# Splitting the late expert weights inside the sampling stage of a fused audio tower

## The chip, the cores and the metric

The kernel runs on one core of a Trainium2 chip. The metric is the device time of one execution in microseconds (us), lower is better; beside it stands the profile of one execution. TensorE multiplies matrices, ScalarE (ACT) and VectorE (DVE) work on columns, GpSimd (POOL) does elementwise work on SBUF, and SyncE (SP) issues DMAs from one queue in program order.

## The reference

```python
h = L0_tok(x)                              # 32 x 166 tokens of 128
h = h + L0_attn(layernorm(h))              # a linear recurrence
h = h + L0_ffn(layernorm(h))               # 16 experts of 512, top 2; an expert's tokens are averaged
h = h + L1_attn(layernorm(h))              # 8 heads; 38 sampled keys choose 25 queries
h = h + L1_ffn(layernorm(h))               # 64 experts of 256, top 42, gelu

# L0_ffn, after the top 2 of the gate (mask, routing_w):
h = silu(einsum('td,efd->tef', x, w1))
h_mean = einsum('tef,te->ef', h, mask) / max(counts, 1)
out = einsum('tk,tkd->td', routing_w, einsum('ef,edf->ed', h_mean, w2)[top_idx])
# L1_ffn, for each expert e of 64:
y = gelu(x @ w1[e] + b1[e]) @ w2[e] + b2[e]     # weighted by comb[:, e] and summed
```

## The kernel before

One core runs five stages one after the other, with a barrier between them: the recurrence, the first mixture (it shares a block with the recurrence), the statistics and sampling of the sparse attention (one block), the attention proper, and the second mixture. Activations lie with their 128 features on the partitions and the 5312 tokens on the columns.

**The weights of the second mixture.** Its 64 experts are held as f16 pairs: a weight is rounded, and what is left of it, scaled up, goes into a second f16 (called splitting below). Experts come in four groups of 16. A group is 8 pieces of 1024 columns (4 for each of the two matrices). Group 0 stays in SBUF; groups 1 to 3 are split early, written to a DRAM buffer (`expert_factors`, kept), and read back in the last stage. Splitting one piece is four operations on GpSimd: round, subtract, scale, add (lines 2202 to 2210 and 2266 to 2274). `ExpertWeights` splits groups 0 and 1 (16 pieces) in the block of statistics and sampling: three pieces beside the statistics, and one after each of the diagonals of chunks 1 to 13. `LateWeights` splits groups 2 and 3 (16 pieces) on GpSimd beside the first mixture. Both have two buffers for raw columns and two for made pairs. The SP queue issues a piece's load as soon as the raw buffer has been read, and its write to DRAM (`sync_keep`) as soon as it is split.

**The first mixture** (`FirstMixture`). The routing has written each token's row to the slots of its two experts in DRAM. 43 tiles of 384 slots follow. For each, SP issues one transposing DMA into a ring of 8 (line 1346), and TensorE makes four blocks of 128 hidden features, each two matmuls of 384 columns (line 1403). Two blocks (768 columns of PSUM) are a set, and four sets are in flight. ScalarE takes silu in place (line 1368), VectorE sums each block over its columns (line 1374). SP also issues, between the transposing loads, the four quarters of the second matrix (after tiles 3, 8 and 13) and, in two of every five tiles, a late load and a late keep, and it waits for GpSimd ahead of each keep. After the last tile come some 30 us of small products that make the outputs.

**Statistics and sampling.** 16 chunks of 332 tokens. The statistics stage makes means and variances chunk by chunk; `rstd` of the first half is ready first. Then for each chunk c GpSimd makes a diagonal of `rstd` (line 1255), TensorE spreads it with one product (line 1261, `pe_spread`), and VectorE normalises. TensorE's work for chunk c is: sampled keys of c, the query and key products of chunk c + 1, the spread of chunk c + 2, and then four times a token-major product of chunk c + 1 and the sampled scores of c. ScalarE copies: query, key, and for each of the four quarters of a chunk three copies of 128 columns (line 1643); its work on chunk c + 1 falls into TensorE's work on chunk c. The sampled keys of c need all four of its quarters copied. Three lines set the order between GpSimd and TensorE:

```python
for c in range(NC):                                  # GpSimd
    norm.pool_diagonal(pool, c, c % 2, stats)        # waits for spread of c - 2
    if 1 <= c <= end - first: k.expert_weights.pool_pieces(pool, first + c - 1, first + c)
```

The block ends for all engines when the last has come to its end, and GpSimd has some constants to make behind its loop (lines 1608 to 1622).

Of the kernel before, what the change touches and what calls it, by code (L numbers as in the profile page):

```python
# [904 lines left out]
def recurrence(nc, k, tables, routing):  # L905
# [8 lines left out]
    with ExitStack() as ctx:  # L914
# [47 lines left out]
        @block.sync  # L962
        def _(sp):
            routing.sync_start(sp)
            for p in range(NC):
                if p >= 2:
                    sp.wait_ge(w_wide, p - 1)
                sp.dma_start(wst[:, p % 2, :], a["w1"][:, p * piece:(p + 1) * piece]).then_inc(raw_in[p % 2], 16)
            routing.sync_fill(sp)
            mixture.sync(sp, y_ready)  # L970

        @block.gpsimd
        def _(pool):
# [19 lines left out]
            mixture.pool(pool)  # L993
# [279 lines left out]
class FirstMixture:  # L1273
# [7 lines left out]
    W2_AT = (3, 8, 13)  # L1281
    KEEP_FROM, KEEP_EVERY = 4, 5

    def __init__(self, nc, k, routing, w_in, w_out, ut, state_of, xc, xsn):
        def sem(name):
# [4 lines left out]
        self.late = LateWeights(nc, k, w_in.rearrange("p a b c d -> p (a b c d)").rearrange("p (j n) -> p j n", j=2),  # L1290
                                w_out.rearrange("p a b c d -> p (a b c d)")[:, 0:2 * PIECE].bitcast(F16).rearrange("p (j q n) -> p j q n", j=2, q=2),
                                states[:, 0:PIECE])
        self.hsum = states[:, PIECE:PIECE + FC * E0 * E0].rearrange("p (f x) -> p f x", f=FC)
        self.ym = states[:, PIECE + FC * E0 * E0:PIECE + FC * E0 * E0 + 128]
        self.part = xc.rearrange("p q c -> p (q c)")[:, 0:NST * FC].rearrange("p (n f) -> p n f", f=FC)
        self.part_t = xsn.rearrange("p q c -> p (q c)")[0:NST, 0:FC * 128]
        self.xt = ut.rearrange("p g i c -> p (g i c)")[:, 0:self.RING * ST].bitcast(F16).rearrange("p (n m t) -> p n m t", n=self.RING, m=2)
# [15 lines left out]
        k.w0_down = k.weights[:, 1].bitcast(F32).rearrange("p a b -> p (a b)")  # L1313
        self.w2 = k.w0_down.rearrange("p (e f d) -> p e f d", e=E0, f=FC)
# [10 lines left out]
    def sync_down(self, sp, q):  # L1325
        es = slice(q * E0 // 4, (q + 1) * E0 // 4)
        sp.dma_start(self.w2[:, es], self.k.a["w2"][:, es]).then_inc(self.k.w2_in, 16)

    def sync(self, sp, outputs_made):
        k, routing, late = self.k, self.routing, self.late  # L1330
        sp.wait_ge(outputs_made, NC)
        late.sync_load(sp, 0)
        late.sync_load(sp, 1)
        sp.wait_ge(k.w0_split, NC)
        self.sync_down(sp, 0)
# [7 lines left out]
        for j in range(NST):  # L1343
# [7 lines left out]
        while late.kept < late.count:  # L1351
# [1483 lines left out]
```

## Time and profile before

| | us |
|---|---|
| median of 3 runs | 2064.61 (2061.93 to 2066.79) |
| the profiled execution, its own time | 2067.39 |
| its span in the trace | 2065.7 |
| first mixture, first tile product to last sum | 283.3 to 397.7 |
| its small products | 397.7 to 428.8 |
| statistics of the third norm | 428.8 to 457.3 |
| sampling | 457.3 to 583.8 |
| attention proper | 583.8 to 718 |
| second mixture | 718 to 2065.7 |

The span is what the trace covers of one execution; the execution's own time is 1.7 us longer. All times in the trace are counted from the start of the span. A wait is shown with the engine and the line that ended it.

### The profile page before, as it was taken

To read this page: it belongs to the slowest core of one execution; us is meant where nothing else is said; L and a number is where in the kernel's file an instruction comes from. 1 tells how busy PE (TensorE), PEld (TensorE's weight loads), DVE (VectorE), ACT (ScalarE), POOL (GpSimd) and SP (SyncE) were. 2 spreads that over 40 slices of the span, in tenths; PEclk is the share of its full clock that TensorE was granted. 3 is DMA by queue.
4 is the path that set the end of the run, shared out by engine and by line. 5 is a ranking of instruction groups with operands and counts; after the bars stand their busy time and mean duration, and the time that the engine had idled before them with its cause. 6 is when DMAs were issued, how large, how long until landed. Compare 5 with 4: busy or idle time off the path is not lost.

```text
span 2065.7 us, 50535 instructions
## 1 busy us (share of the span) xinstructions
PE 1870.1 (91%) x17038; PEld 1349.7 (65%) x17038; DVE 1676.4 (81%) x4833; ACT 1378.0 (67%) x2149; POOL 1455.0 (70%) x1098
## 2 busy tenths in 40 slices
PE   7887436789989978999999999999999999999998
PEld 5555213456669855777777777777777777777776
DVE  5887736555678788899999999999999999999998
ACT  4134525424435545888888888888888888888886
POOL 2216679559800032888888888888888888888887
PEclk9998768789989965999999999999999999999999
DMA  3011289523200010000000200000100000000000
GB/s 93 21 35 63 81 246 257 124 67 94 90 1 1 22 63 1 2 2 0 0 0 3 82 2 0 0 0 35 49 1 0 0 0 2 2 10 11 10 11 19
DMA packets 64334, 77.56 MB, mean 38 GB/s; under 512 B 38932, under 2 KB 47028, under 8 KB 62132
## 3 DMA queue, kind: packets, MB, share of 16 engines
q1 hardware_dynamic: 61364, 70.08, 11.7%
q0 software_dynamic: 2816, 5.45, 0.8%
q8 instruction: 94, 1.54, 0.3%
q14 instruction: 60, 0.49, 0.1%
HBM read 42.97 MB, written 24.08 MB: 32 GB/s over the span
## 4 chain that ended last, share of the span: by engine, by line
PE 58%; DVE 3%; issue 2%; ACT 1%; POOL 0%; ACTq 0%; DVEq 0%; POOLq 0%
PE bank L2679 30%; PE bank L2662 28%; DVE m_work L2553 1%; DVE m_best L2550 1%; DVE m_work L2544 0%; PE bank L2632 0%; DVE m_ut L1269 0%; ACT m_h L2485 0%; DVE m_best L2543 0%; DVE m_ex L2555 0%; DVE h L2591 0%; DVE m_red L2556 0%; DVE m_row L2536 0%; POOL m_diag L1255 0%; ACT m_hidden L2482 0%
## 5 line engine op out<-in xcount | busy, mean ns | idle before, releaser
L2679 PEld LDWEIGHTS bank<-weights,m_h 128*128 128x128 f16 x10752 | 649.6, 98 | 194.4 <-DVE hc L2582 82.6
L2430 POOL TENSOR_TENSOR m_h<-m_hidden,m_h 128x896 f16<-128x896 f32 x384 | 725.9, 1890 | 32.0
L2679 PE MATMUL bank<-weights,m_h 128*128 128x128 f16 x10752 | 724.6, 219 | 10.7 <-POOL m_h L2430 2.1
L2582 DVE SCALAR_TENSOR_TENSOR hc<-bank,m_shares,hc 128x128 f32<-128x128 f32 x2688 | 727.2, 342 | 4.3 <-PE bank L2679 4.3
L2482 ACT ACTIVATE m_hidden<-bank,m_b 128x896 f32<-128x896 f32 x384 | 386.9, 1007 | 197.6 <-PE bank L2662 197.5
L2567 DVE TENSOR_TENSOR m_h<-bank,m_h 128x896 f16<-128x896 f32 x384 | 419.2, 1092 | 116.8 <-ACT m_h L2485 116.7
L2428 POOL TENSOR_SCALAR m_h<-m_hidden 128x896 f16<-128x896 f32 x384 | 360.8, 939 | 117.9 <-ACT m_hidden L2482 99.5
L2662 PE MATMUL bank<-m_u_first,weights 128*128 128x448 f16 (+1 forms) x1536 | 417.8, 354 | 5.5 <-DVE h L2591 5.5
L2662 PE MATMUL bank<-m_u_second,weights 128*128 128x448 f16 (+1 forms) x1536 | 417.7, 354 | 0.0
L2479 ACT ACTIVATE bank<-bank,m_b 128x896 f32<-128x896 f32 x384 | 377.6, 983 | 0.6 <-PE bank L2662 0.6
L2485 ACT ACTIVATE m_h<-bank 128x896 f16<-128x896 f32 x384 | 349.1, 909 | 0.0
L2662 PEld LDWEIGHTS bank<-m_u_second,weights 128*128 128x128 f16 x1536 | 150.8, 98 | 141.4 <-issue 2.0
L699 POOL DMA_INDIRECT expert_slots<-weights,ro_slot x88 | 88.9, 1010 | 76.5 <-DVE weights L839 50.6
L1403 PE MATMUL bank<-lru_ut,weights 128*128 128x384 f16 x344 | 74.1, 373 | 74.5 <-DMA lru_ut<-expert_slots 60.0
L1374 DVE TENSOR_REDUCE lru_xc<-bank 128x2 f32<-128x768 f32 x86 | 77.2, 950 | 67.4 <-ACT bank L1368 67.3
L2662 PEld LDWEIGHTS bank<-m_u_first,weights 128*128 128x128 f16 x1536 | 118.2, 98 | 8.1 <-DVE h L2591 6.4
L1368 ACT ACTIVATE bank<-bank 128x768 f32<-128x768 f32 x86 | 64.7, 798 | 82.6 <-PE bank L1403 82.1
L2399 POOL MEMSET m_row<- 128x96 f32 x1 | 0.2, 178 | 157.0 <-POOLq L1827 157.0
L1403 PEld LDWEIGHTS bank<-lru_ut,weights 128*128 x344 | 37.3, 108 | 110.7 <-issue 99.9
L980 POOL TENSOR_TENSOR lru_diag<-ident,rstd 128x332 f32<-128x332 f32 x16 | 13.5, 858 | 65.3 <-PE bank L1147 41.3
L1711 DVE TENSOR_REDUCE at_peak<-bank 83x8 f32<-83x304 f32 x64 | 30.0, 468 | 35.4 <-PE bank L1769 35.2
L1751 PE MATMUL bank<-at_w_qk,at_ut 128*83 128x384 f32 x128 | 52.9, 501 | 0.0
(359 smaller groups left out, 2153.9 us busy)
## 6 DMA issues: line engine op xcount, KB each, us to landing
weights<-expert_factors SPq DMA_DIRECT2D x12, 1024.0 KB, 8.8
lru_w_in<-e_w_dram SPq DMA_DIRECT2D x16, 512.0 KB, 4.5
expert_factors<-lru_w_out SPq DMA_DIRECT2D x16, 512.0 KB, 4.3
ew_raw<-e_w_dram SPq DMA_DIRECT2D x16, 512.0 KB, 3.9
weights<-w_dram SPq DMA_DIRECT2D x16, 256.0 KB, 2.8
weights<-w_dram SPq DMA_DIRECT2D x4, 1024.0 KB, 6.6
expert_factors<-ew_made SPq DMA_DIRECT2D x8, 512.0 KB, 3.0
xs<-x_dram SPq DMA_DIRECT2D x4, 996.0 KB, 11.8
```

The lines of the kernel that those rows point to most:

```text
L699: g.indirect_dma_start(out=self.k.slots, out_offset=bass.IndirectOffsetOnAxis(ap=self.slot[0:size, q, n:n + 1], axis=0), in_=self.u_tok[0: ...
L1374: v.tensor_reduce(self.part[:, j // PARTS, j % PARTS * FP:(j % PARTS + 1) * FP], self.set_banks(j), X, ALU.add).then_inc(self.summed, 1)
L1403: last = t.matmul(self.set_banks(n)[:, f % FP], self.w0_parts[m][:, bass.ds(expert * FF0 + f * 128, 128)], self.xt[:, j % RING, m], start= ...
L2428: g.tensor_scalar(h1[:, x, 0], hidden[:, x], 1.0 - SHARE, 1.0, ALU.mult, ALU.mult).then_inc(first_of[1], 1)
L2430: g.tensor_tensor(h1[:, x, 1], hidden[:, x], h1[:, x, 0], ALU.subtract).then_inc(second_of[1], 1)
L2479: sc.activation(banks0(x), banks0(x), ACT.Gelu, bias=b1[:, bass.ds(grp * GE + e, 1), 0]).then_inc(gelu[0], 1)
L2482: sc.activation(two(hidden[:, x % 2]), banks1, ACT.Gelu, bias=b1[:, bass.ds(grp * GE + e, 1), 1]).then_inc(gelu[1], 1)
L2485: sc.activation(two(h0[:, x, 0]), banks0(x), ACT.Copy, scale=1.0 - SHARE).then_inc(first_of[0], 1)
L2567: v.tensor_tensor(two(h0[:, x, 1]), banks0(it), two(h0[:, x, 0]), ALU.subtract).then_inc(second_of[0], 1)
L2582: last = v.scalar_tensor_tensor(acc[:, m * TW:(m + 1) * TW], y[q][:, (n - start) * TW:(n - start + 1) * TW], shares[:, m, e:e + 1], acc[:, ...
L2662: last = t.matmul(bank[:, q], k.weights[:, grp % 2, m, at], uu[:, bass.ds(tb * WB + q * HW, HW)], start=(m == 0), stop=(m == 1))
L2679: last = t.matmul(y[q][:, (n - start) * TW:(n - start + 1) * TW], factors[:, m, n * TW:(n + 1) * TW], k.weights[:, grp % 2, 2 + m, at], st ...
```

## The change

Four things change.

1. The 16 late pieces leave GpSimd and the first mixture. They become 32 pieces of 512 columns (`PIECES` goes from 4 to 8 for both classes), two in each of the 16 chunks of the sampling. ScalarE rounds and scales (two operations of 512 columns, after the copies of quarters 1 and 3), VectorE adds (one operation, ahead of the maxima of quarters 0 and 2). They have four raw and four made buffers, two chunks deep, which lie where the squares of the statistics were.
2. The early pieces, now 32 of 512 columns, stay on GpSimd with two buffers each, and all lie in the sampling: two after the diagonal of each chunk from 1 to 15, and two behind the loop. The statistics have none.
3. The second matrix of the first mixture is loaded at once, ahead of the fills of the slots, into four places that are free by then.
4. Of the 86 sets of the first mixture, every sixth (14) is summed by ScalarE, as it takes silu, block by block with an accumulator; VectorE skips it.

The SP queue of the sampling block is rewritten. The core of the diff:

```diff
 # FirstMixture
+    BY_ACT = 6
+    def act_sums(self, n):
+        return n % self.BY_ACT == self.BY_ACT - 1
@@ act
             act.wait_ge(self.up, j + 1)
-            self.nc.scalar.activation(self.set_banks(j), self.set_banks(j), ACT.Silu).then_inc(self.silu, 1)
+            if self.act_sums(j):
+                for f in range(self.FP):
+                    at = j % self.PARTS * self.FP + f
+                    last = self.nc.scalar.activation(self.set_banks(j)[:, f], self.set_banks(j)[:, f], ACT.Silu,
+                                                     accum_out=self.part[:, j // self.PARTS, at:at + 1])
+            else:
+                last = self.nc.scalar.activation(self.set_banks(j), self.set_banks(j), ACT.Silu)
+            last.then_inc(self.silu, 1)
@@ sync
-            if j in self.W2_AT:
-                self.sync_down(sp, 1 + self.W2_AT.index(j))
-            if j >= self.KEEP_FROM and (j - self.KEEP_FROM) % self.KEEP_EVERY in (0, 2):
-                late.sync_keep(sp)
 # sampling block, SP
-                k.expert_weights.sync_pieces(sp, *PIECES_N3)
-                k.expert_weights.sync_pieces(sp, *PIECES_SAMPLE)
+                early, late = k.expert_weights, k.late_weights
+                for s in range(2):
+                    early.sync_load(sp, s)
+                sp.wait_ge(stats.var, NC + DEEP)
+                for i in range(4):
+                    late.sync_load(sp, i)
+                for c in range(NC):
+                    for s in range(2):
+                        late.sync_load(sp, 2 * c + 4 + s)
+                    for s in range(2):
+                        late.sync_keep(sp, 2 * c - 2 + s)
+                    for s in range(2):
+                        early.sync_keep(sp, 2 * c - 2 + s)
+                        early.sync_load(sp, 2 * c + 2 + s)
...
 # sampling block, GpSimd
-                k.expert_weights.pool_pieces(pool, *PIECES_N3)
                 for c in range(NC):
                     norm.pool_diagonal(pool, c, c % 2, stats)
-                    if 1 <= c <= end - first:
-                        k.expert_weights.pool_pieces(pool, first + c - 1, first + c)
+                    if c:
+                        k.expert_weights.pool_pieces(pool, PER_CHUNK * (c - 1), PER_CHUNK * c)
+                k.expert_weights.pool_pieces(pool, PER_CHUNK * (NC - 1), PER_CHUNK * NC)
-PIECES = 4
+PIECES = 8
+PIECES_POOL, PIECES_LATE = (0, 2 * GROUP), (2 * GROUP, NG * GROUP)
+PER_CHUNK = 2
 # LateWeights, new
+    def sync_load(self, sp, i):
...
+        if i >= 4:
+            sp.wait_ge(self.raw_read, i - 3)
+        start = n // GROUP * GE * HC * 128 + n % PIECES * PIECE
+        sp.dma_start(self.raw[:, i % 4, :], src[:, start:start + PIECE]).then_inc(self.raw_in[i % 4], 16)
+    def act_piece(self, act, c, j, s):
+        b = 2 * j + s
+        act.wait_ge(self.raw_in[b], 8 * c + 16 - 8 * j)
+        if not isinstance(c, int) or c >= 2:
+            act.wait_ge(self.kept_out[b], 8 * c - 8 * j)
+        self.nc.scalar.activation(self.made[:, b, 0], self.raw[:, b], ACT.Copy).then_inc(self.rounded, 1)
+        if not isinstance(c, int) or c:
+            act.wait_ge(self.split, 2 * c + s - 1)
+        self.nc.scalar.activation(self.wide[:, s], self.raw[:, b], ACT.Copy, scale=1.0 / SHARE).then_inc(self.raw_read, 1)
+    def dve_piece(self, dve, c, j, s):
+        b = 2 * j + s
+        dve.wait_ge(self.rounded, 2 * c + s + 1)
+        dve.wait_ge(self.raw_read, 2 * c + s + 1)
+        self.nc.vector.scalar_tensor_tensor(self.made[:, b, 1], self.made[:, b, 0], 1.0 - 1.0 / SHARE, self.wide[:, s], ALU.mult,
+                                            ALU.add).then_inc(self.split, 1)
```

The waits of the early pieces are as before: `ExpertWeights.sync_load(n)` waits until piece n - 2 has been subtracted, `sync_keep(n)` (from n = 16 on, the second group) until piece n is split, and GpSimd's piece n (from n = 18 on) until the keep of piece n - 2 has landed.

## Rows read from the trace of the kernel before

**Rows 1.** The first line of the page.
```profile
span 2065.7 us, 50535 instructions
```

**Rows 2.** Busy time by stretch: stretch, length, engines, clock, DMA share, GB/s.
```profile
283.30:397.70 114.40, 74.07 (x344) 37.26 (x344) 77.16 (x86) 64.69 (x86) 95.66 (x61) 0.84 0.96 238
...
428.80:457.30 28.50, 20.99 (x155) 16.87 (x156) 15.61 (x31) 9.18 (x19) 21.42 (x16) 0.84 0.35 102
...
457.30:583.80 126.50, 122.59 (x495) 75.16 (x493) 76.15 (x218) 53.42 (x226) 99.13 (x75) 0.97 0.25 79
```

**Rows 3.** Timeline of the DMA queue SP, first mixture: start, length, what.
```profile
330.41 0.38 SPq L2253 DMA_DIRECT2D expert_factors<-lru_w_out  x1
...
330.92 3.74 SPq L1346 DMA_TRANSPOSE lru_ut<-expert_slots  x2
...
337.44 4.24 SPq L1346 DMA_TRANSPOSE lru_ut<-expert_slots  x3
...
343.47 0.38 SPq L2253 DMA_DIRECT2D expert_factors<-lru_w_out  x1
```

**Rows 4.** Timeline of the first mixture, its tiles back to back.
```profile
283.29 7.67 PE L1403 MATMUL bank<-lru_ut,weights 128*128 128x384 f16 x32 [36.04 <-DMA lru_ut<-expert_slots]
...
287.35 4.44 ACT L1368 ACTIVATE bank<-bank 128x768 f32<-128x768 f32 x6 [0.48 <-PE bank L1403]
...
309.67 2.77 PE L1403 MATMUL bank<-lru_ut,weights 128*128 128x384 f16 x16 [3.09 <-DMA lru_ut<-expert_slots]
...
335.70 9.69 DVE L1374 TENSOR_REDUCE lru_xc<-bank 128x2 f32<-128x768 f32 x11 [0.32 <-ACT bank L1368]
```

**Rows 5.** Lines of ScalarE before the first mixture: busy, mean ns, idle before.
```profile
L764 ACT ACTIVATION_READ_ACCUMULATOR weights<-weights 128x1 f32 x44 | 8.5, 193 | 0.0
```

**Rows 6.** The transposing loads, line 1346: ns min/median/max, first and last start.
```profile
L1346 SPq DMA_TRANSPOSE lru_ut<-expert_slots x43: 1205/1347/2764, 280.2 to 389.6; - x43
```

**Rows 7.** Timeline, from the statistics to the first sampling chunk.
```profile
455.00 1.44 POOL L1255 TENSOR_TENSOR at_diag<-ident,rstd 128x332 f32<-128x332 f32 x2
...
455.89 2.55 PE L1261 MATMUL bank<-at_diag,ones 128*128 128x332 f32 x4 [4.96 <-POOL at_diag L1255]
```

**Rows 8.** Timeline of chunks 8 and 9 of the sampling, ScalarE and TensorE.
```profile
525.07 0.27 ACT L1643 ACTIVATE at_kx<-bank 83x128 f32<-83x128 f32 x1
...
527.06 0.72 PE L1261 MATMUL bank<-at_diag,ones 128*128 128x332 f32 x2
...
532.41 0.27 ACT L1643 ACTIVATE at_kx<-bank 83x128 f32<-83x128 f32 x1
```

**Rows 9.** Timeline of GpSimd and SP in the same chunks.
```profile
528.05 0.74 POOL L1255 TENSOR_TENSOR at_diag<-ident,rstd 128x332 f32<-128x332 f32 x1
...
528.12 0.38 SPq L2183 DMA_DIRECT2D expert_factors<-ew_made  x1
...
535.28 0.74 POOL L1255 TENSOR_TENSOR at_diag<-ident,rstd 128x332 f32<-128x332 f32 x1
```

**Rows 10.** Lines of GpSimd: a tensor_tensor of 512 columns.
```profile
L163 POOL TENSOR_TENSOR lru_on_diag<-ident,lru_factor 128x512 f32<-128x512 f32 x4 | 4.0, 1042 | 17.9 <-DVE lru_factor L263 17.9
```

**Rows 11.** DMA issues of the page: KB each, median us to landing.
```profile
weights<-w_dram SPq DMA_DIRECT2D x16, 256.0 KB, 2.8
...
expert_factors<-ew_made SPq DMA_DIRECT2D x8, 512.0 KB, 3.0
```

**Rows 12.** The same splitting of 512 columns in the recurrence: ScalarE, VectorE.
```profile
L1008 ACT ACTIVATE weights<-weights 128x512 f32<-128x512 f32 x16 | 9.9, 616 | 5.9 <-DVE weights L1092 5.9
...
L1092 DVE SCALAR_TENSOR_TENSOR weights<-weights x16: 676/683/1146, 101.7 to 224.0; 128x512 f16<-128x512 f16 x16
```

**Rows 13.** Timeline, end of the sampling block and start of the attention.
```profile
551.14 0.15 POOL L1608 IOTA at_uline<- 83x25 f32 x1
...
555.69 4.14 POOL L1622 TENSOR_SCALAR_AFFINE_SELECT at_expand<-at_expand 128x3200 bf16<-128x3200 bf16 x1
...
583.88 0.32 PE L2030 MATMUL bank<-ch_rank,at_expand 128*100 128x166 bf16 x2 [0.32 <-PEq L1534]
```

More of the change, by code:

```diff
@@ L992, in _ @@
             mixture.pool_clear(pool)
-            mixture.pool(pool)
         @block.scalar
@@ L1326, in sync_down, with sync_second, sync @@
         es = slice(q * E0 // 4, (q + 1) * E0 // 4)
-        sp.dma_start(self.w2[:, es], self.k.a["w2"][:, es]).then_inc(self.k.w2_in, 16)
-    def sync(self, sp, outputs_made):
-        k, routing, late = self.k, self.routing, self.late
+        sp.dma_start(self.w2[q], self.k.a["w2"][:, es]).then_inc(self.k.w2_in, 16)
+    def sync_second(self, sp, outputs_made):
         sp.wait_ge(outputs_made, NC)
[L1332 to L1335, printed above, removed]
+        sp.wait_ge(self.k.w0_split, NC)
+        for q in range(4):
+            self.sync_down(sp, q)
+    def sync(self, sp):
+        k, routing = self.k, self.routing
         sp.wait_ge(routing.rows_made, 1)
@@ L1358, in pool_clear @@
         g.memset(self.ym[:], 0.0).then_inc(self.cleared, 1)
-    def pool(self, pool):
-        for i in range(self.late.count):
-            self.late.pool_piece(pool, i)
     def act(self, act):
@@ L1592, in _ @@
                 sp.dma_start(w_o[:], a["wo"]).then_inc(small_in, 16)
-                k.expert_weights.sync_pieces(sp, *PIECES_N3)
-                k.expert_weights.sync_pieces(sp, *PIECES_SAMPLE)
+                early, late = k.expert_weights, k.late_weights
[12 more added lines that the diff above has]
+                        early.sync_load(sp, 2 * c + 2 + s)
+                for s in range(2):
+                    late.sync_keep(sp, 2 * NC - 2 + s)
+                    early.sync_keep(sp, 2 * NC - 2 + s)
+                late.sync_kept(sp)
+                early.sync_kept(sp)
             @block.gpsimd
@@ L2183, in sync_keep, with sync_kept @@
         sp.dma_start(self.k.kept[n // GROUP - 1, :, 2 * mat:2 * mat + 2, cols], self.made[:, n % 2]).then_inc(self.k.kept_out[n % 2], 16)
-    def sync_pieces(self, sp, first, end):
-        self.sync_load(sp, first)
-        for n in range(first, end):
-            if n + 1 < end:
-                self.sync_load(sp, n + 1)
-            self.sync_keep(sp, n)
-        if end == 2 * GROUP:
-            for p in range(2):
-                sp.wait_ge(self.k.kept_out[p], 16 * GROUP // 2)
+    def sync_kept(self, sp):
+        for p in range(2):
+            sp.wait_ge(self.k.kept_out[p], 16 * GROUP // 2)
     def pool_pieces(self, pool, first, end):
```

101 lines of the change are left out of this document (46 added, 55 removed).

## The prediction, made before the change was run

> **What bounds the kernel now.** I read the stages first, by busy time in each stretch: three of them carry the change [rows 2]. The first mixture takes 114.4 us, and no compute engine that it needs is full in it (TensorE 74, VectorE 77, ScalarE 65); only GpSimd, whose work there is the late pieces, is busy for 96. The timeline of the DMA queue shows why: two keeps later, five tiles later, 13.06 us have gone by [rows 3], so 2.61 us a tile and 43 tiles in 112. SP waits for GpSimd's split ahead of each keep, and the next transposing loads stand behind that wait. The stage goes by GpSimd, through SP's program order. Fed back to back its own engines are faster: 11 sums of VectorE in 9.69 us, 0.87 a set; 6 silus of ScalarE in 4.44 us, 0.73 a set; 16 products in 2.77 us, 0.69 a set [rows 4].
>
> The sampling is TensorE's: 122.6 of 126.5 us [rows 2]. Call K(c) the moment when ScalarE has copied the last quarter of chunk c, S(c) the spread of chunk c. K(8) is 525.34, S(10) is 527.06, K(9) is 532.68 [rows 8]: so K to S 1.7, S to the next K 5.6, a chunk 7.34. GpSimd does a diagonal and a 1024 piece in 7.23 us and never stops [rows 9]; it keeps up because SP has nothing else to do than to serve it.
>
> **First mixture.** Without GpSimd's pieces five sets in six cost ScalarE 0.73, the sixth two activations of 384 columns (0.5 each, between half of a set's and the 0.62 of 512 columns [rows 12]) and two reads of the accumulator at 0.19 [rows 5]: 1.4. That is 5.05 for six, 0.84 a set, 72 us for 86. VectorE has 72 sets at 0.87, 63 us. The transposing loads cost SP 1.35 each, 58 us [rows 6]. ScalarE is the bound. The first 32 products took 7.67 us where the warm rate makes 5.5 [rows 4]; that start, 2.1 us, stays. 74 us against 114.4: **-40 us**. Bounds: 0.78 a set (-45), and 0.9 (-35). The early second matrix goes at some 225 us, while SP waits for the routing: nothing, and nothing is lost if it doesn't, since the matrix is wanted last.
>
> **Statistics.** TensorE stood 4.96 us for the first diagonals, which GpSimd reached only at 455.00, behind its third piece [rows 7]. This piece goes away: **-6 us** (5 by the row, a little more because VectorE's constants no longer run beside it; bounds -4 and -8).
>
> **Sampling, the work.** Per chunk ScalarE gets four operations of 512 columns at 0.62 and VectorE two at 0.68 [rows 12]. Both are idle for over a third of the stage (53 and 76 busy of 126.5 [rows 2]), so this costs at most some tenths in a chunk; I take 0.1. A GpSimd piece of 512: two tensor_tensors at 1.04 [rows 10], two light operations near half of a 1024's, gaps: 3.4 us (bounds 3.28, half of a 1024, and 3.6). A pair 6.8, with the diagonal 7.5. By itself that would just about do.
>
> **Sampling, the waits.** SP now serves two masters in one order. In its round c it first issues late loads 2c + 4 and 2c + 5; the second waits until ScalarE has read piece (c, 1), two operations after K(c): K + 1.25. Behind it stand two late keeps, early keep 2c - 2, early load 2c + 2, early keep 2c - 1, early load 2c + 3. So nothing for GpSimd leaves SP before K(c) + 1.25 + 0.5 + 0.9 = K + 2.65 (an issue is 0.38 to 0.5 [rows 9]).
>
> *Rounds up to 8.* GpSimd's pieces 2c + 2 and 2c + 3 stand ahead of diagonal c + 3. Their load is issued at K(c) + 2.65 and lands 2.8 later [rows 11], or 2.95 with the three transfers just ahead of it: K + 5.6. Pieces 6.8, diagonal 0.75, signal 0.1: S(c + 3) = K(c) + 13.25. Due is K(c) + 9.04 (K(c + 1) + 1.7). K(c + 2) = S(c + 3) + 5.6 = K(c) + 18.9: 9.4 a chunk instead of 7.34.
>
> *Rounds 9 to 13.* From piece 18 on GpSimd's piece 2c also waits for the landing of keep 2c - 2, which SP issues in round c, after K(c). But piece 2c stands ahead of diagonal c + 2, and S(c + 2) is due at K(c) + 1.7. Now the circle goes round in one chunk. Keep 2c - 2 is issued at K + 2.65 and lands at K + 5.3 (3.0 for double the bytes [rows 11]); piece 2c until K + 8.7. Early load 2c + 2 waits until that piece is subtracted (K + 7.05), early keep 2c - 1 goes behind it at K + 7.6 and lands at K + 10.2; piece 2c + 1 until K + 13.6; diagonal and signal K + 14.45 = S(c + 2). Then 5.6, and 2.1 because TensorE comes from a wait of 12.7 us: the start after a wait of 36 us cost 2.1 [rows 4], 1.2 instead of 2.4 GHz. K(c + 1) = K(c) + 22.15, three times a chunk of before. Five chunks: 111 us instead of 37.
>
> Of this clock: the start at 283.29 ran slow (32 products at 0.24 us each) and 16 products after 3.09 us of idle did not (0.17 each) [rows 4]. The Trainium skill says the same of such a pattern (TensorE: Matmul & The Clock Gate, HAM oscillation — how this bites in real kernels: a kernel whose matmuls come in bursts with waits between them starts each burst at half clock). By that rule the term of 2.1 stands five times, 10 us; if the clock held, the sum would be 10 less.
>
> *Sum.* K(0) was 525.34 - 8 x 7.34 = 466.6; it comes to 461.2 (-6, and 0.6 for the first ScalarE piece). K(1) = +7.4. K(9) = K(1) + 4 x 18.9 = 544.2. K(14) = 655. GpSimd then has pieces 28 and 29 (until K + 13.6), 30 and 31 (SP's keep of 28 stands behind load 31, issued at K + 12.0, and two late keeps; it lands near K + 16; end K + 22.8), and its constants, 551.14 to 559.83, 8.7 us [rows 13]. These were hidden under three chunks of TensorE; now they end last: K + 31.8 = 686.8. The attention began at 583.88 [rows 13]: **+103 us**, the 6 us of the statistics counted in. Bounds: landing 0.6 less, pieces 3.28, no clock term: 9.2 and 19.2 a chunk, +86. Landing 1 us more, pieces 3.6, and 3 us for the clock: 10 and 25 a chunk, +125.
>
> **Behind it** nothing changes: the attention and the second mixture have the same instructions.
>
> **Sum.** The profiled execution took 2067.4 us around its span of 2065.7 [rows 1]; -40 + 103 makes 2130; the median of the runs shown is 2.8 lower: **2127 us**, 3.0% slower. Own range: 2064.6 - 45 + 86 = 2106 to 2064.6 - 35 + 125 = 2155.
>
> **Rivals.**
> - *Only the loads bind.* The keeps are in time, because GpSimd runs further ahead of TensorE than I say, or its second group goes differently. Then 9.4 a chunk throughout: K(14) = 461.2 + 7 x 18.9 - 0.9 (round 0 has no keeps ahead of its loads) = 592.6, S(15) near 587, then two pairs of pieces with a short wait, and the constants: 614, so +30, total 2064.6 - 40 + 30 = 2055. For: the loads' wait needs only SP's order, the keeps' wait the position of the pieces as well. Against: diagonal c + 2 stands behind piece 2c in GpSimd's program. 7%.
> - *Neither binds, the change gains (other side).* One mechanism: late load 2c + 5 leaves SP early, ScalarE's pieces being ahead of the quarters they follow; it decides from the point where round c is issued 6 us before K(c). Then GpSimd's 7.5 hides under 7.34 plus the slack won in the statistics, TensorE ends 6 us earlier, and GpSimd's tail at 575 to 580: total 2064.6 - 40 - 5 = 2020. For: SP is free for most of a chunk before. Against: ScalarE's order is fixed, copies first. 6%.
> - *The first mixture doesn't get faster*: TensorE stays at the low clock (twice 0.69 a set, 86 x 1.38 = 119 us), or the transposing loads take the 2.76 us that the slowest took [rows 6]. The gain of 40 is gone: 2167. For: the start of the stage. Against: 16 products in 2.77 us after an idle 3.09 [rows 4]. 5%.
> - *The change doesn't take its hold*, no difference: 2%.
>
> **Chances.** The forecast 80%. A measurement of this kernel can tell about 0.2%, 4 us. Slower 85%, same 2%, faster 13%. Range, 8 in 10: the own range, reaching a little towards the loads' rival and to the slow first mixture: 2098 to 2158.
>
> **What would show it.** The first mixture from 283.3 to near 357, VectorE's sums 72. The first spread near 450. In the sampling, GpSimd waits for a DMA load of its raw columns in chunks 3 to 9, and for `expert_factors` from chunk 11 on, some 8 us in two waits a chunk; TensorE waits for line 1255 by 11 to 13 us in five chunks; SP waits for ScalarE in its late load. GpSimd's constants end last before the attention, near 685. The forecast is wrong if spreads keep a pitch below 10 us after chunk 10, if the first mixture ends after 370, or if ScalarE or VectorE, not line 1255, hold TensorE.

## The result: 3.9% slower, and the profile after

The changed kernel takes 2145.56 us (median of 4 runs, 2141.85 to 2148.54), the kernel before 2064.28 in the same runs: a ratio of 1.0393 (95% interval 1.0372 to 1.0413), +81.3 us. The profiled execution took 2148.54 us, with a span of 2146.8.

Busy time by stage, from the trace of the kernel after; the columns are those of [rows 2]. The stages are the first mixture, its small products, the statistics, and the sampling in three stretches (to the diagonal of chunk 9, the rounds with early keeps, the tail):

```profile
core 0: us, PE busy (x) PEld busy (x) DVE busy (x) ACT busy (x) POOL busy (x), PEclk, DMA share, GB/s
284.80:369.00 84.20, 68.61 (x344) 35.06 (x345) 64.32 (x72) 66.59 (x128) 0.00 (x0) 0.91 0.51 97
369.00:398.00 29.00, 26.71 (x168) 19.80 (x168) 8.91 (x17) 0.00 (x0) 0.00 (x0) 0.94 0.00 1
398.00:416.80 18.80, 18.58 (x152) 15.13 (x153) 10.52 (x31) 9.27 (x19) 3.47 (x6) 0.99 0.14 44
416.80:510.41 93.61, 69.21 (x248) 40.66 (x247) 46.93 (x111) 43.28 (x147) 61.84 (x70) 0.86 0.47 140
510.41:640.16 129.75, 56.46 (x182) 31.71 (x182) 35.22 (x99) 31.72 (x108) 46.82 (x55) 0.70 0.32 93
640.16:681.14 40.98, 20.20 (x68) 11.30 (x69) 14.85 (x41) 9.86 (x36) 23.98 (x27) 0.71 0.29 94
```

In the stretch 510 to 640 no engine is busy for half of the time and TensorE's clock is at 0.70: everything waits. Who waits for whom is in the grouped waits of the sampling, 440 to 700 us of the same trace (us in total, times, longest):

```profile
PE bank L1261 <- POOL at_diag L1255: 97.4, 9, 15.0
POOL ew_made L2232 <- DMA expert_factors<-ew_made: 95.4, 13, 15.1
POOL weights L2232 <- DMA ew_raw<-e_w_dram: 19.2, 4, 6.5
```

TensorE waits for diagonals, GpSimd, which makes them, for its keeps (95 us) and its loads (19 us; one more wait of 8.7 us for a load lies ahead of this window). The moments K(c), read from ScalarE's fourth copy of each chunk, tell the rhythm: in the kernel before they lie 7.34 apart, from 466.70; after they are 427.08, 434.32, 447.92, 455.31, 471.69, 479.36, 495.22, 502.61, 519.04, 526.42, 550.33, 574.27, 600.00, 624.56, 648.70.

**A round with loads only**, K(4) = 471.69. The SP queue, GpSimd, TensorE and ScalarE of the trace after, to be read beside [rows 8] and [rows 9]:

```profile
470.41 2.67 SPq L2273 DMA_DIRECT2D lw_room<-e_w_dram  x2
473.12 0.94 SPq L2281 DMA_DIRECT2D expert_factors<-lw_room  x2
474.11 1.16 SPq L2212 DMA_DIRECT2D ew_raw<-e_w_dram  x2
...
478.71 0.61 POOL L2232 CAST weights<-ew_raw 128x512 f16<-128x512 f32 x1 [6.01 <-DMA ew_raw<-e_w_dram]
486.65 0.74 POOL L1255 TENSOR_TENSOR at_diag<-ident,rstd 128x332 f32<-128x332 f32 x1
...
487.44 1.48 PE L1261 MATMUL bank<-at_diag,ones 128*128 128x332 f32 x2 [6.19 <-POOL at_diag L1255]
488.71 1.49 PE L1784 MATMUL bank<-at_w_qk,at_ut 128*83 128x384 f32 x2
...
494.95 0.27 ACT L1672 ACTIVATE at_kx<-bank 83x128 f32<-83x128 f32 x1
```

SP stands in the late load until ScalarE has read its piece, issues the early load at K + 2.4, and GpSimd has it at K + 7.0. Two pieces and the diagonal follow, TensorE starts its spread at K + 15.75, and K(6) is 495.22: 23.5 us for two chunks.

**A round with early keeps**, K(11) = 574.27, same trace:

```profile
572.99 2.67 SPq L2273 DMA_DIRECT2D lw_room<-e_w_dram  x2
575.70 0.95 SPq L2281 DMA_DIRECT2D expert_factors<-lw_room  x2
576.69 0.53 SPq L2219 DMA_DIRECT2D expert_factors<-ew_made  x1
582.80 0.34 SPq L2212 DMA_DIRECT2D ew_raw<-e_w_dram  x1
583.19 0.43 SPq L2219 DMA_DIRECT2D expert_factors<-ew_made  x1
...
580.93 0.61 POOL L2232 CAST ew_made<-ew_raw 128x512 f16<-128x512 f32 x1 [14.03 <-DMA expert_factors<-ew_made]
586.62 0.61 POOL L2232 CAST ew_made<-ew_raw 128x512 f16<-128x512 f32 x1 [1.90 <-DMA expert_factors<-ew_made]
590.36 0.74 POOL L1255 TENSOR_TENSOR at_diag<-ident,rstd 128x332 f32<-128x332 f32 x1
...
591.25 1.44 PE L1261 MATMUL bank<-at_diag,ones 128*128 128x332 f32 x2 [14.96 <-POOL at_diag L1255]
```

The first keep leaves at K + 2.4 and has landed at K + 6.7; the load waits behind it for GpSimd's subtraction, the second keep behind the load; it has landed at K + 12.35, the diagonal comes at K + 16.1, the spread at K + 17.0.

### The profile page after: what moved, and what is told of

Read it like the earlier page. It is cut to its first block, busy times and chain, and to the rows that moved or that the text cites. A ratio compares the mean times of both kernels' runs of the same rounds, so it can differ in the third digit from the quotient of the medians.

```text
span 2146.8 us, 50790 instructions
## 1 busy us (share of the span) xinstructions
PE 1878.4 (87%) x17038; PEld 1342.6 (63%) x17038; DVE 1678.8 (78%) x4851; ACT 1410.6 (66%) x2255; POOL 1369.0 (64%) x1098
## 4 chain that ended last, share of the span: by engine, by line
PE 56%; DVE 3%; issue 2%; ACT 1%; POOL 0%; ACTq 0%; DVEq 0%; POOLq 0%
PE bank L2707 28%; PE bank L2690 27%; DVE m_work L2581 1%; DVE m_best L2578 0%; PE bank L2660 0%; DVE m_work L2572 0%; DVE m_ut L1269 0%; ACT m_h L2513 0%; DVE m_best L2571 0%; DVE m_ex L2583 0%; DVE h L2619 0%; POOL m_h L2458 0%; DVE m_red L2584 0%; ACT m_hidden L2510 0%; DVE m_row L2564 0%
## 5 line engine op out<-in xcount | busy, mean ns | idle before, releaser
L2707 PEld LDWEIGHTS bank<-weights,m_h 128*128 128x128 f16 x10752 | 639.2, 98 | 190.0 <-DVE hc L2610 103.1
L1413 PE MATMUL bank<-lru_ut,weights 128*128 128x384 f16 x344 | 68.6, 348 | 48.6 <-DMA lru_ut<-expert_slots 35.1
L1672 ACT ACTIVATE weights<-bank 83x128 f32 (+1 forms) x64 | 17.5, 273 | 141.1 <-PE bank L1784 141.1
L1261 PE MATMUL bank<-at_diag,ones 128*128 128x332 f32 x32 | 19.3, 707 | 97.4 <-POOL at_diag L1255 97.4
L1384 DVE TENSOR_REDUCE lru_xc<-bank 128x2 f32<-128x768 f32 x72 | 64.3, 951 | 48.7 <-ACT bank L1375 48.7
L1375 ACT ACTIVATE bank<-bank 128x768 f32<-128x768 f32 x72 | 54.2, 798 | 48.9 <-PE bank L1413 48.5
```

Of the source, the lines that this page charges most:

```text
L1384: v.tensor_reduce(self.part[:, j // PARTS, j % PARTS * FP:(j % PARTS + 1) * FP], self.set_banks(j), X, ALU.add).then_inc(self.summed, 1)
L1413: last = t.matmul(self.set_banks(n)[:, f % FP], self.w0_parts[m][:, bass.ds(expert * FF0 + f * 128, 128)], self.xt[:, j % RING, m], start= ...
L2707: last = t.matmul(y[q][:, (n - start) * TW:(n - start + 1) * TW], factors[:, m, n * TW:(n + 1) * TW], k.weights[:, grp % 2, 2 + m, at], st ...
```

## The experiments

Each edits the kernel after, unless it says otherwise. The span from chunk to chunk is the pitch of GpSimd's diagonals (line 1255), read from GpSimd's timeline. It is given for the rounds without early keeps (two of them together, where they alternate; the first such pair, in which the queues start, is left out) and with them.

| run | median us | ratio to before | without keeps | with keeps |
|---|---|---|---|---|
| after | 2145.56 | 1.0393 | 23.2 to 23.8 for two | 23.3 to 25.2 |
| late loads a round later | 2113.94 | 1.0267 | 19.7 to 21.1 for two | 20.3 to 21.5 |
| early keeps first | 2083.20 | 1.0091 | 22.3 to 23.8 for two | 25.1 to 26.5 for two |
| keeps, then loads | 2063.19 | 0.9998 | 18.1 to 19.4 for two | 11.5 to 13.9 |
| both late transfers a round later | 2074.86 | 1.0048 | 8.9 to 9.2 | 14.6 to 15.4 |
| both, and the new order | 2043.44 | 0.9899 | 8.9 to 9.2 | 9.5 to 9.9 |

### What SP's order costs

**Late loads one round later.**

```diff
-                for i in range(4):
+                for i in range(2):
                     late.sync_load(sp, i)
...
-                        late.sync_load(sp, 2 * c + 4 + s)
+                        late.sync_load(sp, 2 * c + 2 + s)
```

> The changed kernel with the late loads issued one round later (two at the start instead of four, then 2c + 2 and 2c + 3 in round c), so that SP is held by ScalarE's chunk c - 1 and no longer by chunk c. Nothing else, all the split pieces stay where they are. Theory of SP's order: both circles open; GpSimd's own work paces, 8.5 us a chunk (two pieces and a diagonal in the changed kernel's trace), 10.6 from chunk 11 on, where keep 2c - 1 still stands behind a load; the attention begins near 570 instead of 681 and the whole takes about 2035 us. Rival, the added work of ScalarE and VectorE beside TensorE is what costs: the spreads stay more than 15 us apart after chunk 10, the whole above 2100. Rival, the traffic of 96 smaller transfers costs: landings above 4 us remain, the whole between 2070 and 2110.

2113.94 us (ratio 1.0267, interval 1.0216 to 1.0318): 32 us won, far less than expected. SP's queue, VectorE and GpSimd in its trace say why:

```profile
544.67 0.91 SPq L2273 DMA_DIRECT2D lw_room<-e_w_dram  x2
545.62 9.09 SPq L2281 DMA_DIRECT2D expert_factors<-lw_room  x2
554.76 0.48 SPq L2219 DMA_DIRECT2D expert_factors<-ew_made  x1
...
553.62 0.69 DVE L2301 SCALAR_TENSOR_TENSOR lw_room<-lw_room 128x512 f16<-128x512 f16 x1
...
557.38 0.92 POOL L2232 CAST ew_made<-ew_raw 128x512 f16<-128x512 f32 x1 [10.49 <-DMA expert_factors<-ew_made]
```

The late load no longer holds SP, but the late keep behind it does, for 9 us: it waits for VectorE's second piece, which stands behind the maxima of two quarters, and so behind the next chunk's spread. There were two waits of one kind in a row, and I had seen only the first. By the marks set ahead (over 15 us apart, over 2100 us) this result fell on the side of the rival that the added work itself costs. The rows above speak for the queue, but what settles it is a later version, with both late transfers lagged and a new order: it has all the added work and takes 2043.44 us.

**Early keeps at the head of the round.**

```diff
+                    for s in range(2):
+                        early.sync_keep(sp, 2 * c - 2 + s)
                     for s in range(2):
                         late.sync_load(sp, 2 * c + 4 + s)
...
-                        early.sync_keep(sp, 2 * c - 2 + s)
                         early.sync_load(sp, 2 * c + 2 + s)
```

> The changed kernel with the early keeps at the head of each round, ahead of the late loads; the early loads stay behind them. Theory: only the circle of one chunk opens (rounds 9 to 13, 24.4 us each), the circle of the loads over two chunks stays: 23.3 us for two chunks all the way. Five chunks times 12.7 us are saved: the attention begins near 617, the whole about 2082 us. If the waits for the landing of the keeps were an effect of traffic and not of the order, it stays near 2145.

2083.20 us (1.0091, 1.0071 to 1.0111). That is the 2082 us expected. The one-chunk circle of the keeps is undone, and what is left is the two-chunk circle throughout; GpSimd still waits 18.9 us for early loads, and 29.4 us for keeps instead of 95.4. This one move gives back 62 us.

**Keeps first, then loads, of both kinds.**

```diff
                     for s in range(2):
-                        late.sync_load(sp, 2 * c + 4 + s)
+                        early.sync_keep(sp, 2 * c - 2 + s)
                     for s in range(2):
                         late.sync_keep(sp, 2 * c - 2 + s)
                     for s in range(2):
-                        early.sync_keep(sp, 2 * c - 2 + s)
                         early.sync_load(sp, 2 * c + 2 + s)
+                    for s in range(2):
+                        late.sync_load(sp, 2 * c + 4 + s)
```

> SyncE's order in each sampling round becomes: both early keeps, both late keeps, both early loads, both late loads (as changed: late loads, late keeps, then early keep, load, keep, load). The trace with the late loads one round later still had a circle of 20.6 us a chunk, because VectorE's second piece of a chunk is computed only behind the scores of the next chunk, and GpSimd's keeps were queued behind that late keep; the trace with the keeps first still waited 18.9 us for early loads, queued behind late ones. Theory that the whole loss is the order on SyncE's queue: with both in front, diagonal to diagonal is GpSimd's own work, 8.5 us, and in the rounds with early keeps about 9.2 us (the keep of piece 2c-2 goes out 6.5 us behind a diagonal and lands 3.4 us later). Last diagonal about 537 us, attention about 561 us, total about 2027 us. Rival, that the pieces' own work and transfers cost as much (ScalarE's 2.1 us a chunk in the circle, landings longer in the crowd): pitch stays over 11 us, total over 2060 us.

2063.19 us (0.9998, 0.9989 to 1.0008): as fast as the kernel before, but 36 us short of the expectation. Its SP queue stood for up to 10.0 us in the pair of late keeps of a round (from 526.74 on), for the reason of the first run. Here, too, the rival's marks (over 11 us, over 2060 us) were met, and the same later version decides.

**Both late transfers one round later, order unchanged.**

```diff
-                        late.sync_load(sp, 2 * c + 4 + s)
+                        if c:
+                            late.sync_load(sp, 2 * c + 2 + s)
...
-                        late.sync_keep(sp, 2 * c - 2 + s)
+                        late.sync_keep(sp, 2 * c - 4 + s)
```

(The last four late keeps follow behind the loop, here and in the next version; these lines are left out.)

> The kernel after with nothing changed but the index of SyncE's late transfers, both one round later (loads of chunk c+1, keeps of chunk c-2), the order within a round as it was (late loads, late keeps, then keep, load, keep, load of the early pieces). Theory: the two-chunk circle is gone, and in the rounds with early keeps the second keep still goes out behind a load that waits for the next chunk's piece, lands 5.7 us behind the next diagonal where 4.5 us are wanted: about 9.7 us a chunk there, total about 2040 us. Rival (the order within the round is needed too): rounds of 12 us or more, total over 2065 us.

2074.86 us (1.0048, 1.0032 to 1.0064). The two-chunk circle is gone (9.0 a chunk), but the rounds with keeps take 14.6, not 9.7: the rival was right there. SP and GpSimd in its trace:

```profile
538.48 0.35 SPq L2214 DMA_DIRECT2D ew_raw<-e_w_dram  x1
538.87 0.91 SPq L2275 DMA_DIRECT2D lw_room<-e_w_dram  x2
539.82 0.94 SPq L2283 DMA_DIRECT2D expert_factors<-lw_room  x2
540.81 0.54 SPq L2221 DMA_DIRECT2D expert_factors<-ew_made  x1
547.14 0.34 SPq L2214 DMA_DIRECT2D ew_raw<-e_w_dram  x1
547.53 0.43 SPq L2221 DMA_DIRECT2D expert_factors<-ew_made  x1
...
545.27 0.61 POOL L2234 CAST ew_made<-ew_raw 128x512 f16<-128x512 f32 x1 [4.18 <-DMA expert_factors<-ew_made]
550.92 0.61 POOL L2234 CAST ew_made<-ew_raw 128x512 f16<-128x512 f32 x1 [1.87 <-DMA expert_factors<-ew_made]
```

Each keep stands behind a load that waits for the next piece (538.48, 547.14), so a keep of a piece that has long been split leaves late and GpSimd waits for its landing twice a round. The late transfers of these rows don't wait for anything (538.87 to 540.76), they only take 1.9 us to issue: with this order the early pieces bind themselves.

**Both late transfers one round later, and early keeps, late keeps, late loads, early loads.**

```diff
                     for s in range(2):
-                        late.sync_load(sp, 2 * c + 4 + s)
+                        early.sync_keep(sp, 2 * c - 2 + s)
                     for s in range(2):
-                        late.sync_keep(sp, 2 * c - 2 + s)
+                        late.sync_keep(sp, 2 * c - 4 + s)
+                    for s in range(2):
+                        if c:
+                            late.sync_load(sp, 2 * c + 2 + s)
                     for s in range(2):
-                        early.sync_keep(sp, 2 * c - 2 + s)
                         early.sync_load(sp, 2 * c + 2 + s)
```

> The run with the late keeps second in each round still had rounds of 11.5 to 13.9 us, and SyncE held 8 to 10 us on the late keeps: GpSimd's diagonal of chunk c goes with ScalarE's and VectorE's pieces of chunk c-1, and VectorE's second piece of chunk c-2 is computed 8 us behind that diagonal, behind the scores. So here both late transfers are issued one round later, where their waits are over (late keeps of chunk c-2, late loads of chunk c+1), in the order early keeps, late keeps, late loads, early loads. Theory (order and lag on SyncE's queue are the whole loss): pitch of the diagonals 8.5 us in rounds without early keeps, at most 9 with them; last diagonal near 535 us, attention about 31 us later near 566 us, total about 2034 us. Rival (the transfers' crowd or the pieces themselves): pitch over 10 us with waits for landed loads or keeps that were issued in time, total over 2050 us.

2043.44 us (0.9899, 0.9883 to 0.9916): 21 us faster than the kernel before, with all of the change's work in place. It is 9 us more than expected: the rounds are half a microsecond longer than the 8.5 taken for GpSimd's own work, and those with early keeps 1.0 to 1.4 us. In its trace SP waits mainly in the early loads, and GpSimd's wait for keeps is down to 0.6 to 1.9 us a round:

```profile
533.26 1.95 SPq L2222 DMA_DIRECT2D expert_factors<-ew_made  x2
535.25 1.01 SPq L2284 DMA_DIRECT2D expert_factors<-lw_room  x2
536.30 1.46 SPq L2276 DMA_DIRECT2D lw_room<-e_w_dram  x2
538.40 4.46 SPq L2215 DMA_DIRECT2D ew_raw<-e_w_dram  x2
...
546.38 0.61 POOL L2235 CAST ew_made<-ew_raw 128x512 f16<-128x512 f32 x1 [0.78 <-DMA expert_factors<-ew_made]
```

What is left of the loss is in GpSimd's own work. Two pieces of 512 columns take 7.47 us undisturbed, where one of 1024 took 6.55 before. And some of its operations take longer than the others of their form, as this one in the trace after (the same cast takes 0.61 us elsewhere), each time while VectorE adds a late piece:

```profile
482.44 1.07 POOL L2232 CAST weights<-ew_raw 128x512 f16<-128x512 f32 x1
...
481.83 1.22 DVE L2301 SCALAR_TENSOR_TENSOR lw_room<-lw_room 128x512 f16<-128x512 f16 x1
```

Of GpSimd's 144 operations on pieces and diagonals, 11 were so lengthened after (3.9 us in all) and 29 in this version (12 us), and in all 40 VectorE's addition was running. VectorE's additions took up to 1.56 us instead of 0.68, too. So the added work does cost something once the waits are gone; no run here takes it apart further.

**Constants and first pieces ahead.** Two versions were meant to take GpSimd's tail away. One edits the kernel after: constants and pieces 0 and 1 ahead of the first diagonal, every round's pieces one chunk earlier, the SP order early load, early keep, early load, early keep, late loads, late keeps, and the experts' numbers 22 at a time. The other is the version just shown with the constants ahead of the first diagonal.

> A version meant to beat both kernels: GpSimd makes the constants of the attention part and its first two pieces ahead of the first diagonal, where it waits 14.3 us, so each round's pieces come one chunk earlier; SyncE's order is early load, early keep, early load, early keep, then late loads, late keeps; the experts' numbers of the first mixture are read 22 tiles at a time. If GpSimd's own work bounds the rounds: 8.5 us from diagonal to diagonal in all of them, last diagonal near 534 us, behind it only 7.5 us of pieces, which lie beside the 20 us from the last spread to attention: attention near 554 us, total near 2018 us. If the order was not all of it: rounds over 10 us, total over 2040 us.

> As the run with the shifted order, and GpSimd makes the constants of the attention part ahead of its first diagonal, in the 14 us in which it waits there, in place of behind its last piece. If GpSimd's last work sets the start of the attention part, attention comes 9 us earlier (near 557 us) and the total is about 2025 us; if the path over the last spread (20 us from the last spread to attention in the kernel before) sets it, less.

The first took 2082.81 us (1.0089) instead of some 2018: its late transfers are the unlagged ones and stand ahead of the next round's early load, and GpSimd waited 30.1 us for early loads in four waits of up to 10.4, and 31.9 us for early keeps in four of up to 8.8. The second took 2042.96 us (0.9894, 0.9877 to 0.991), the same as without it (2043.44): from the first product of the first mixture to the attention it needs 290.4 us instead of 293.7, 3.3 less and not 9, and the total doesn't show them.

### What the first mixture gained

**VectorE makes all sums.** `act_sums` is False for every set, `dve_sets` counts all.

> The changed kernel with every set of the first mixture summed by VectorE. In the changed kernel six sets took some 4.7 us; with 86 sums of 0.88 us six take 5.3: the first mixture is 8 us longer (84 to 92 us), the whole near 2153 us. If TensorE or the transposing loads set the pace there, no difference.

2151.08 us, ratio 1.042. From the first to the last product of the stage 86.7 us instead of 81.7 after; 112.0 before. So, with the late pieces gone, the sums by ScalarE are worth 5 us (8 were expected), and the rest of the change to this stage (the late pieces taken out, the second matrix loaded ahead) 25.

**The same sums, but the pieces left where they were** (an edit of the kernel before).

> The kernel before with one part of the change alone: ScalarE sums every sixth set of the first mixture, all pieces where they were. Before, TensorE also waited 19 us for tiles of tokens behind the first in this stage, which more sums by ScalarE don't shorten: the stage gets at most 5 us shorter (what the sums were worth in the kernel after), the total 2059 to 2064 us. The loop of the second mixture took 1239.8 us before and 1223 to 1226.5 us in the eight kernels with the change, with the tiles moved too: if it is what stands in the late parts of the program that sets it, it stays at 1240 us; if how the engines stand to each other when the loop begins, it may come out either way.

2066.95 us (1.0013, 1.0003 to 1.0023). The stage's products take 110.7 us instead of 112.0, and TensorE waits for landed tiles of tokens as before (61.1 us in 13 waits, 36.1 of them ahead of the first). Alone, this part is worth nothing.

**The experts' numbers 22 tiles at a time.** TensorE reads the number of each tile's expert into a register, 16 tiles at a time (`load_rows`); in the trace after, these stops are the rows "issue":

```profile
317.84 7.17 PE L1413 MATMUL bank<-lru_ut,weights 128*128 128x384 f16 x32 [5.68 <-issue]
...
348.39 9.10 PE L1413 MATMUL bank<-lru_ut,weights 128*128 128x384 f16 x40 [4.18 <-issue]
```

```diff
-            if j % 16 == 0:
-                experts = load_rows(self.nc, pe, routing.owner_i[0:1, j:min(j + 16, NST)], 0, E0 - 1)
-            expert = experts[j % 16]
+            if j % 22 == 0:
+                experts = load_rows(self.nc, pe, routing.owner_i[0:1, j:min(j + 22, NST)], 0, E0 - 1)
+            expert = experts[j % 22]
```

> The changed kernel with the experts' numbers of the first mixture read into TensorE's registers 22 tiles at a time instead of 16, so once instead of twice within the stage. Theory: each read stops TensorE for 5.7 us and the matmuls behind it start at the lower clock, some 1.5 us more; the first mixture is 7 us shorter (84 to 77 us). Rival, the stops are the tiles' loads and only fall together with the reads: no difference.

2146.38 us, the same as after (2145.56), and 81.0 us from first to last product instead of 81.7. Two stops became one that is as long as both together, in the trace of this run:

```profile
329.33 7.56 PE L1413 MATMUL bank<-lru_ut,weights 128*128 128x384 f16 x32 [10.85 <-issue]
```

The kernel before has both stops too, 5.58 us at 330.81 and this one:

```profile
370.96 9.81 PE L1403 MATMUL bank<-lru_ut,weights 128*128 128x384 f16 x40 [4.35 <-issue]
```

The stop moved with the reads, so it is theirs and not the tiles'. Fewer and longer calls save nothing: 9.9 us for 27 numbers in two stops after (0.36 and 0.38 each), 10.85 for 21 in one stop here (0.52 each). Why a number costs more here isn't shown; the reads themselves have no rows in the traces.

### The 15 us of the last stage

From its first to its last product the loop of the second mixture took 1239.8 us before and 1225.1 after, with the same instructions. Of TensorE's timeline three experts' first products in the kernel before, and then in the kernel after:

```profile
1320.07 1.06 PE L2679 MATMUL bank<-weights,m_h 128*128 128x128 f16 x16
...
1323.36 1.05 PE L2679 MATMUL bank<-weights,m_h 128*128 128x128 f16 x16
...
1326.43 1.06 PE L2679 MATMUL bank<-weights,m_h 128*128 128x128 f16 x16
```

```profile
1422.49 1.05 PE L2707 MATMUL bank<-weights,m_h 128*128 128x128 f16 x16
...
1425.62 1.05 PE L2707 MATMUL bank<-weights,m_h 128*128 128x128 f16 x16
...
1428.76 1.05 PE L2707 MATMUL bank<-weights,m_h 128*128 128x128 f16 x16
```

It is a rhythm of two experts: before, the steps from expert to expert are 3.29 and 3.07 us in turn, together 6.36; after, 3.13 and 3.14, together 6.27. How the 6.27 are shared between the two varies along the stage, the sum hardly does, and each kernel keeps its own (TensorE is busy for 100.00 of 100 us in every window from 1000 to 1700 after, for 99.25 to 99.44 from 900 to 1600 before). Two runs looked for what chooses it.

> The kernel after, with 10 KB a partition left free ahead of the tiles of the second mixture, so that these lie where they lay before (the buffers of the early pieces are 10 KB smaller after). The loop of the second mixture took 1239.8 us before and 1223 to 1225 us in all five kernels that have the change, whatever else was altered. Theory that the place of the tiles in the memory makes it: the loop takes about 1240 us again and the total rises by 15 us to about 2160 us. Rival, that it has another cause (the place of the instructions in memory, the semaphores): the loop stays at 1223 to 1226 us and the total at 2145 us.

2146.29 us, loop 1225.5 us: the place of the tiles is not it.

> The kernel before with 49 instructions more on ScalarE and 31 more on VectorE (copies of one column into a tile that nothing reads) at the start of the attention block, so that on these two engines the second mixture's instructions lie as far from the start of the program as in the kernel after; nothing else is changed. The loop of the second mixture took 1240 us in the kernel before and with its first mixture changed alone, and 1223 to 1227 us in all ten kernels that have the rest of the change, with the tiles moved, with TensorE's program one instruction shorter, and with 0.1 us to 3 us between the first products. Theory that the place of ScalarE's and VectorE's instructions sets its rhythm: the loop takes about 1225 us here, the total falls by some 5 to 15 us (the copies may cost up to 10). Rival, something else of the kernel before (GpSimd's program, or a state left by the late pieces): it stays at 1240 us, the total at 2065 to 2075 us.

2074.15 us, loop 1238.8 us: nor is the place of ScalarE's and VectorE's instructions. (The total is longer because the copies delay the statistics: from the first mixture's last sum to the first spread 66.4 us, 58.3 before.) The loop took 1223.0 to 1225.9 us in the kernel after and the ten edits of it, and 1238.8 to 1240.8 in the kernel before and the two edits of that. So the first mixture's sums are not it either, nor when the stage begins (809 to 917 us). What of the rest it is (GpSimd's program ahead of the loop, SP's, or the state in which the sampling leaves something) stays open.

## Why the prediction was right, and where its sizes were off

The forecast was 2127 us and slower; it came to 2145.56, by the mechanism named, the two circles through SP's order. That the number fell into the range took luck, as the last point shows. The span came out at 2146.8 where the prediction's sum makes 2065.7 - 40 + 103 = 2128.7. Point by point:

- **First mixture, -40, came to -31** (28.7 up to the last sum, 2.1 in its small products, a gain that I had not counted; the stage began 1.5 us later and was 30.2 shorter). 84.2 us, less the 2.1 of the slow start and the two stops of 5.68 and 4.18, is 72.2 for 86 sets, the forecast 0.84 a set. That is partly chance: between the stops six sets took 4.62 to 4.89 us of ScalarE's time, 0.79 a set, and the remaining 4 us lie at the slow starts behind the stops and at the last set's end (an estimate from these figures). What failed is the sum, which left out TensorE's register reads. Both stops stood in the trace before, 5.58 and 4.35 us, among the waits of that stage. The result lies outside my bound of -35.
- **Statistics, -6, came to -8.3** (27.1 to 18.8 us up to the first spread): just beyond the bound of -8.
- **Rounds up to 8, 18.9 us for two chunks, came to 23.0** (K(1) to K(9) is 92.1 for four pairs, 20.8 in the first and 23.5 to 23.8 in the others): +16.5 in all. The circle was as described; mis-sized, in the round shown, were the load, in GpSimd's hands 7.0 us behind K instead of 5.6 (4.6 behind its issue instead of 2.95), the pieces at 3.73 and 4.2 instead of 3.4 each, and S to K, 7.8 instead of 5.6: I charged the slow clock only where TensorE waits 12.7 us, but after waits of 6 to 7 us its spread took 1.48 us instead of 0.72, too.
- **Rounds 9 to 13, 22.15 each, came to 24.5** (K(9) to K(14), 122.3): +11.5. Mis-sized was the landing of the keeps, the first 6.7 instead of 5.3 behind K, and the pieces again (3.74 each), so that K to S was 16.7 in the mean (17.0 in the round shown) instead of 14.45. S to K with the slow clock, 5.6 + 2.1, came to 7.8 (mean of five): right.
- **The tail, K(14) + 31.8, came to 32.4**: GpSimd's constants did end last (its last row begins at 676.65 and takes 4.14, the attention starts at 681.14).
- **Behind it nothing changes** failed: the second mixture came out some 15 us faster, which hid almost half of the errors above (9.2 and 28.0 more, less 2.3, make 34.9; less the 16.1 behind the start of the attention and 0.7 of small terms, they make the 18.1 between the spans). Without it the median would have been 2160, outside the range. No step of the prediction foresaw this, and its cause is open: it is luck.

The waits that I named as signs are there: line 1261 waits for GpSimd by up to 15.0 us, GpSimd for `expert_factors` twice a chunk, SP in its late load. Three signs were wrongly worked out. "Some 8 us in two waits a chunk" doesn't follow from my own round, which leaves GpSimd idle for 13.1 and 1.5 us; the trace has 14.0 and 1.9. And the first spread "near 450" and the last constants "near 685" leave out the 40 us that the first mixture was to give; with them they would be 410 and 645. Measured are 416.8 and 680.8, so the second agrees with what I wrote only because the errors above add up to some 35 us by there. Against the rivals: "only the loads bind" is ruled out by the 95 us for keeps; "neither binds" needs the late transfers out of the way, and the version that has this (2043 us) shows what it is worth, less than the rival's 2020, because GpSimd's rounds take 8.9 to 9.9 us and not 7.3. The slow first mixture did not come: its clock was 0.91.

Of the transfers, the same early load on the pages before and after:

```profile
ew_raw<-e_w_dram SPq DMA_DIRECT2D x16, 512.0 KB, 3.9
...
ew_raw<-e_w_dram SPq DMA_DIRECT2D x32, 256.0 KB, 3.1
```

Half the bytes took 0.8 us less. The early keep took 3.0 us with 512 KB before [rows 11] and 3.4 with 256 KB after, where it stands behind two late keeps. So halving the pieces bought little per transfer and doubled their number. The Trainium skill (DMA: Bandwidth & Descriptors, Anatomy of one DMA — SWDGE (gpsimd) path) fits a fixed cost of about 2 us and a part by the bytes for transfers issued by GpSimd; that most of the time is fixed agrees with these loads of SP, where half the bytes make 0.8 of 3.9 us; the keeps don't show a part by the bytes.

Of the clock: after each of its nine waits for a diagonal, of 4.1 to 15.0 us, TensorE's first products ran at about half speed (1.44 to 1.49 us against 0.72 to 0.81 of the same form), and the stretch with waits of 14 to 15 us was granted 0.70. The Trainium skill (TensorE: Matmul & The Clock Gate, HAM oscillation — how this bites in real kernels) says that of bursts with waits between them; the trace agrees, and it held in the rounds with the shorter waits as well. With still shorter waits it went either way: of four spreads after some 3 us in the run with the late loads a round later three took 0.80 to 0.83 us and one 1.47, and in the best version one of seven after 1.7 to 2.0 us took 1.45.

What makes the good version 25.1 us shorter in its span (2040.6): 0.9 and 40.6 up to the first spread and 15.4 in the last stage, 1.8 between, less 33.7 in the sampling (161.7 us against 128.0). Without the unexplained part it would be ahead by 10 in these two traces, and by 6 in the medians.

## What to carry to other kernels

One in-order DMA queue that serves two masters needs each transfer placed where its wait is already over; write down for every issue which engine's step it waits for and at what point of the round that step comes, and lag its index by a round where it comes late. Undo the waits of such a queue one at a time and the next one takes over: lagging the load alone gave back 32 us here, both lags 71, the order alone 82, and lags and order together 102. When a stage gets faster, look for the stops that were hidden under its old rhythm, such as register reads.

## What the runs showed of the hardware

- Reading numbers from SBUF into TensorE's registers cost 0.36 to 0.52 us a number (5.68 us for 16, 4.18 for 11, 10.85 for 21), and TensorE stood meanwhile, however the reads were grouped.
- GpSimd's operations on pieces and diagonals (0.61 to 1.15 us) took 0.3 to 0.5 us longer in 40 cases in two traces, and in all 40 VectorE's addition of two SBUF operands was running beside them; of the operations that it overlapped, about half were lengthened.
- The same loop, with the same instructions, ran in one of two steady rhythms, 1.2% apart in time (1240 and 1225 us), each kept through the stage; a change in another part of the program moved it from one to the other. Comparisons of parts of a kernel should be made by stage, or such a jump is put down to the edit.
